# Forty-eight of 108 expert tiles computed while the token pipeline drains

## What is computed

```python
tokens = einsum('bnpd,edp->bne', patches(x, P=16, S=8), Wr) + b      # 93 tokens a row
h = tokens + attention(layernorm(tokens))                            # 8 heads of 64, causal, ALiBi
x2 = layernorm(h).reshape(-1, 128)                                   # 5952 tokens
top_vals, top_idx = top_k(x2 @ gate_weight.T, 2)
mask  = any(top_idx == e)                                            # token chose expert e
hid   = silu(einsum('td,efd->tef', x2, w1))                          # 16 experts, 512 hidden
h_mean = einsum('tef,te->ef', hid, mask) / max(counts, 1)
y_mean = einsum('ef,edf->ed', h_mean, w2)
out = h + softmax(top_vals) mixed over y_mean[top_idx]
```

## Time and profile before

| | us |
|---|---|
| median of 3 runs (lowest to highest) | 823.14 (822.13 to 823.62) |
| the profiled execution | 821.97 |
| its span, first to last instruction | 820.3 |
| TensorE busy in the span | 742.3 (90%) |
| VectorE busy | 615.6 (75%) |
| ScalarE busy | 468.0 (57%) |
| GpSimd busy | 383.2 (47%) |

### The profile page before, as it was taken

One profiled execution on the slowest core, in us unless ns is written; L12 is line 12 of the kernel. 1 busy time (PEld: TensorE's weight loads), 2 busy tenths in 40 slices (PEclk: granted clock), 3 DMA queues, 4 the chain that ended last, 5 costly groups with the idle time before them and its releaser, 6 DMA issues. The chain is left out here.

```text
span 820.3 us, 20971 instructions
## 1 busy us (share of the span) xinstructions
PE 742.3 (90%) x6670; PEld 685.7 (84%) x6670; DVE 615.6 (75%) x1621; ACT 468.0 (57%) x1021; POOL 383.2 (47%) x408
## 2 busy tenths in 40 slices
PE   5477999999999999999999999999898419999987
PEld 4466999999999999999999999998777309999983
DVE  2145788888888888888888888889986336888855
ACT  3345566656565656666566666646443108899950
POOL 3443243666555565656456565644534552222200
PEclk9798999999999999999999999999999659999989
DMA  6322123432211121112111121142000032222205
GB/s 190 105 76 54 42 67 97 135 100 52 67 50 48 47 63 51 50 47 67 51 47 47 47 71 48 32 158 77 13 13 20 20 81 73 65 64 64 64 12 149
DMA packets 42246, 53.89 MB, mean 66 GB/s; under 512 B 13651, under 2 KB 28947, under 8 KB 41680
## 3 DMA queue, kind: packets, MB, share of 16 engines
q1 hardware_dynamic: 26304, 37.13, 16.0%
q0 software_dynamic: 13120, 14.05, 6.1%
q10 hardware_dynamic: 2768, 2.00, 0.8%
HBM read 42.69 MB, written 10.26 MB: 65 GB/s over the span
## 5 line engine op out<-in xcount | busy, mean ns | idle before, releaser
L1110 POOL DMA_INDIRECT expert_rows<-hn,slot x128 | 167.5, 1309 | 64.3 <-issue 32.3
L1043 POOL TENSOR_TENSOR x_lo<-x_raw,x_hi 128x752 fp32r<-128x752 f32 x64 | 114.9, 1796 | 149.1 <-ACT x_hi L667 149.1
L831 DVE SCALAR_TENSOR_TENSOR qkv<-ps,taps,qkv 128x368 f32<-128x368 f32 x192 | 114.0, 594 | 76.8 <-ACT qkv L675 75.3
L675 ACT ACTIVATE qkv<-ps,taps 128x372 f32<-128x372 f32 x192 | 108.7, 567 | 87.5 <-PE ps L408 87.1
L834 DVE SCALAR_TENSOR_TENSOR qkv<-ps,taps,qkv 128x364 f32<-128x364 f32 x192 | 114.6, 597 | 6.8
L406 PE MATMUL ps<-x_hi,wtok_hi 128*128 128x376 f32 x256 | 94.5, 369 | 11.5 <-DVE wtok_lo L811 9.1
L500 PEld LDWEIGHTS psO<-vrow,probT 93*93 93x93 f32 x1024 | 93.4, 162 | 4.9 <-ACT probT L700 3.8
L500 PE MATMUL psO<-vrow,probT 93*93 93x65 f32 x1024 | 93.9, 245 | 2.2 <-ACT probT L700 1.1
L407 PE MATMUL ps<-x_lo,wtok_hi 128*128 128x376 f32 x256 | 88.3, 345 | 0.0
L408 PE MATMUL ps<-x_hi,wtok_lo 128*128 128x376 f32 x256 | 88.3, 345 | 0.0
L998 DVE TENSOR_REDUCE qkv<-qkv 128x512 f32 (+1 forms) x108 | 72.4, 681 | 18.1 <-ACT qkv L771 17.3
(11 more groups left out here) (160 smaller groups left out, 1607.1 us busy)
## 6 DMA issues: line engine op xcount, KB each, us to landing
x_raw<-in_x SPq DMA_DIRECT2D x64, 376.0 KB, 3.2
w1s<-in_w POOLq DMA_DIRECT2D x8, 512.0 KB, 4.8
w<-in_w SPq DMA_DIRECT2D x4, 1024.0 KB, 10.3
xs<-expert_rows SPq DMA_DIRECT2D x54, 64.0 KB, 1.8
xs<-expert_rows POOLq DMA_DIRECT2D x54, 64.0 KB, 2.1
out<-resid SPq DMA_DIRECT2D x16, 160.0 KB, 2.4
expert_rows<-hn,slot POOLq DMA_INDIRECT x128, 3.5
qkv<-in_w_tok ACTq DMA_DIRECT2D x4, 256.0 KB, 6.7
```

The source lines that it names most:

```text
L675: nc.scalar.activation(qkv[u][:, k, :, :], psP[(k + 1) % 2][:, 0:GT].rearrange("p (b n) -> p b n", n=NT), ACT.Copy, scale=taps[:, k, 2:3]) ...
L831: nc.vector.scalar_tensor_tensor(dst[:, :, 1:NT], src[:, :, 0:NT - 1], taps[:, k, 1:2], dst[:, :, 1:NT], ALU.mult, ALU.add).then_inc(tap1_ ...
L1043: nc.gpsimd.tensor_tensor(x_lo[u][:, 0:PIECE], x_raw[u][:, :], x_hi[u][:, 0:PIECE].bitcast(F32), ALU.subtract)\
L1110: nc.gpsimd.indirect_dma_start(rows, bass.IndirectOffsetOnAxis(slot[1 - u][:, c:c + 1], 0), hn[1 - u][:, c % GB, :], None)\
```

## The change

`EARLY` = 48 tiles are computed before the second part. After eleven groups (`FULL_AFTER`) the ranks tell how many full tiles each expert has already; VectorE makes a first table of these in step 15 (`early_piece`), TensorE turns it into a row in step 16, and VectorE copies it to `tab_e`. The 48 tiles are worked in twelve quads of four. Quads 0 to 3 stand in the sub-steps of step 18, 4 to 6 in step 19, and 7 to 11 (`LAST_QUADS`) after the pipeline's last step. All 48 are fetched by SP alone (`fetch_early`), from the end of the projections on, since buffers share memory with the projection's. For the same reason the last megabyte of w2 is loaded then. A quad has one bank for its four transposes and one copy (`quad_copy`), and two score banks (`psP`), which the drain leaves free, where the second part has four. The final table, five operations longer, leaves out the tiles done and numbers the other 60 from 48 on.

```diff
@@ constants and buffers @@
+ROUND, QUAD = 12, 4
+FULL_AFTER = 11
+EARLY = 48
...
+        xs = [sb(f"xs{k}", [128, D]) for k in range(NR)]
+        xsQ = [sb(f"xsQ{u}", [D, QUAD * 128]) for u in range(2)]
+        xsT = [xsQ[0][:, k * 128:(k + 1) * 128] for k in range(NX)]
@@ fetch_early @@
+        def fetch_early(eng):
+
+            eng.wait_ge(early_table, 1)
+            for u in range(2):
+                eng.wait_ge(scattered[u], 16 * 2 * GB * ((FULL_AFTER + 1 - u) // 2))
+
+            def fetch(i, k):
+                start = eng.value_load(tab_e[0:1, bass.ds(i, 1)], min_val=0, max_val=E * CAP)
+                wait(eng, xs_tr, i - (NR - 1))
+                eng.dma_start(xs[k][:, :], rows[bass.ds(start, 128), :]).then_inc(xs_early[k], 16)
+
+            for k in range(NR):
+                fetch(k, k)
+            with eng.Fori(1, EARLY // NR) as r:
+                for k in range(NR):
+                    fetch(r * NR + k, k)
+
@@ expert, quads @@
         def expert(eng, copy, i, k, done):
 
-            at = eng.value_load(tab[0:1, bass.ds(i + 128, 1)], min_val=0, max_val=(E - 1) * F)
+            table = tab_e if isinstance(i, int) and i < EARLY else tab
+            at = eng.value_load(table[0:1, bass.ds(i + 128, 1)], min_val=0, max_val=(E - 1) * F)
             wait_apart(eng, up_mm, i - (NX - 1))
             copy(wtile[k % NX][:, :], w1s[:, bass.ds(at, F)]).then_inc(done, 1)
+
+        def early_quad(t, s):
+
+            return isinstance(t, int) and t >= NG + 2 and {(NG + 2, 0): 0, (NG + 2, 1): 1, (NG + 2, 2): 2, (NG + 2, 3): 3,
+                                                          (NG + 3, 0): 4, (NG + 3, 2): 5, (NG + 3, 3): 6}.get((t, s), -1)
+
+        LAST_QUADS = range(7, EARLY // QUAD)
+
+        def quad(t, s):
+
+            q = early_quad(t, s)
+            return None if q is False or q < 0 else q
@@ SP @@
             sp.wait_ge(tap_mm, NPIECE)
-            for j in range(FB):
+            for j in range(FB - 1):
                 sp.dma_start(w2s[j][:, :, :], w2[:, j, :, :]).then_inc(late_w_in, 16)
             sp.wait_ge(zeros_ready, 1)
             sp.dma_start(rows[E * CAP:ROWS, :], zeros[:, :]).then_inc(zero_tile_out, 16)
+            sp.wait_ge(proj_mm, NG * NBLK)
+            sp.dma_start(w2s[FB - 1][:, :, :], w2[:, FB - 1, :, :]).then_inc(late_w_in, 16)
+            fetch_early(sp)
             sp.wait_ge(tail_ready, 1)
             tails(sp, 0)
             fetch_tiles(sp, 0)
@@ TensorE @@
+            def turn_quad(q):
+
+                wait(pe, xs_evac, QUAD * q)
+                for c in range(QUAD):
+                    i = q * QUAD + c
+                    pe.wait_ge(xs_early[i % NR], 16 * (i // NR + 1))
+                    nc.tensor.transpose(psTok[:, c * 128:(c + 1) * 128], xs[i % NR][:, :], ident[:, :]).then_inc(xs_tr, 1)
+
+            def up_quad(q, first, count):
+
+                for c in range(first, first + count):
+                    i = q * QUAD + c
+                    weights_ready(i // ROUND, i % ROUND)
+                    pe.wait_ge(xs_evac, QUAD * (q + 1))
+                    wait(pe, silu_done, i - 1)
+                    if i < 2:
+                        pe.wait_ge(conv_done, NG * NBLK)
+                    for j in range(FB):
+                        mm = nc.tensor.matmul(psP[i % 2][:, j * 128:(j + 1) * 128], wtile[i % NX][:, j * 128:(j + 1) * 128],
+                                              xsQ[q % 2][:, c * 128:(c + 1) * 128], start=True, stop=True)
+                    mm.then_inc(up_mm, 1)
...
+                    if q is not None and (f.attn or s == 0):
+                        turn_quad(q)
                     if prev:
 
                         pe.wait_ge(p_evac, n * 2)
@@ -527,6 +605,8 @@
                         proj(t, u, f, 3 * s + 1)
                     if f.tok:
                         tok_taps(t, s, 1, 2)
+                    if q is not None and f.attn:
+                        up_quad(q, 0, 3)
                     if f.attn and prev:
                         pe.wait_ge(v_evac, n + 1)
...
+                    if q is not None and f.attn:
+                        up_quad(q, 3, 1)
                     if prev:
...
@@ -583,25 +679,29 @@
             pe.wait_ge(tcol_ready, 1)
             pe.wait_ge(rwT_evac, NG)
             for c in range(2):
-                mm = nc.tensor.matmul(psTok[0:1, c * 128:(c + 1) * 128], tcol[:, c:c + 1], ident[:, :],
+                mm = nc.tensor.matmul(psV[0:1, c * 128:(c + 1) * 128], tcol[:, c:c + 1], ident[:, :],
                                       start=True, stop=True)
             mm.then_inc(table_mm, 1)
+            for q in LAST_QUADS:
+                if q == LAST_QUADS[0]:
+                    turn_quad(q)
+                up_quad(q, 0, 2)
+                if q + 1 in LAST_QUADS:
+                    turn_quad(q + 1)
+                up_quad(q, 2, 2)
+            pe.wait_ge(table_ready, 1)
@@ ScalarE @@
+            def quad_copy(q):
+
+                ac.wait_ge(xs_tr, QUAD * (q + 1))
+                wait(ac, up_mm, QUAD * (q - 1))
+                nc.scalar.activation(xsQ[q % 2][:, :], psTok[:, :], ACT.Copy).then_inc(xs_evac, QUAD)
+
+            def silu_quad(q, first, count):
+
+                for c in range(first, first + count):
+                    i = q * QUAD + c
+                    ac.wait_ge(up_mm, i + 1)
+                    wait(ac, tile_sum, i - (NX - 1))
+                    nc.scalar.activation(act[i % NX][:, :], psP[i % 2][:, :], ACT.Silu).then_inc(silu_done, 1)
+                    if i + NX < EARLY and copies(i + NX):
+                        expert(ac, lambda d, w: nc.scalar.activation(d, w, ACT.Copy), i + NX, i + NX, w_act_ready)
...
+                    q = quad(t, s)
+                    if q == 0:
+                        ac.wait_ge(early_table, 1)
+                        ac.wait_ge(expert_w_in, 16 * 2 * GB)
+                        ac.wait_ge(v_tr, (NG - 1) * GB)
+                        ac.wait_ge(s_mm, (NG - 1) * GB)
+                        for k in range(NX):
+                            if copies(k):
+                                expert(ac, lambda d, w: nc.scalar.activation(d, w, ACT.Copy), k, k, w_act_ready)
...
+                    if q is not None and (f.attn or s < 3):
+                        quad_copy(q)
+                        if f.attn:
+                            silu_quad(q, 0, 3)
...
+                    if q is not None and f.attn:
+                        silu_quad(q, 3, 1)
+                    if q is not None and not f.attn and s < 3:
+                        silu_quad(q, 0, QUAD)
                     if f.gate and s == 3:
                         wait(ac, gap_done, t - 3)
                         nc.scalar.activation(egap[:, :], gap[:, :], ACT.Exp).then_inc(egap_done, 1)
+                    if q is not None and not f.attn and s == 3:
+                        quad_copy(q)
+                        silu_quad(q, 0, QUAD)
...
             run(ac, step)
             ac.wait_ge(tail_ready, 1)
             tails(ac, 1)
+            for q in LAST_QUADS:
+                if q == LAST_QUADS[0]:
+                    quad_copy(q)
+                silu_quad(q, 0, 2)
+                if q + 1 in LAST_QUADS:
+                    quad_copy(q + 1)
+                silu_quad(q, 2, 2)
@@ VectorE @@
+            def sum_quad(q):
+
+                for c in range(QUAD):
+                    i = q * QUAD + c
+                    tile_total(i, i % NX)
+                    if i + NX < EARLY and not copies(i + NX):
+                        expert(dve, nc.vector.tensor_copy, i + NX, i + NX, w_dve_ready)
...
+                    if f.gate and s == 3 and not f.attn:
+                        sum_quad(quad(t, 2))
                     if f.gate and s == 3:
                         rank(t - 4, u)
                     if f.proj:
                         conv(t, u, 3 * s + 1)
                     if f.proj:
                         conv(t, u, 3 * s + 2)
+                    if q is not None and f.attn:
+                        if q == 0:
+                            first_weights()
+                        sum_quad(q)
                     if prev:
                         dve.wait_ge(out_mm, n)
                         res = resid[:, bass.ds((n - 1) * D, D)]
                         nc.vector.tensor_tensor(res, psWout, res, ALU.add).then_inc(res_add, 1)
                     if f.gate and s == 2:
                         route(t - 4)
+                    if isinstance(t, int) and t == NG - 1:
+                        early_piece(s)
+                    if isinstance(t, int) and t == NG and s == 2:
+                        dve.wait_ge(early_mm, 1)
+                        nc.vector.tensor_copy(tab_e[:, :], psTok[0:1, 0:2 * 128]).then_inc(early_table, 1)
...
+            link(nc.vector.reciprocal(invc[:, :], invc[:, :]))
+            sum_quad(LAST_QUADS[0] - 1)
             dve.wait_ge(table_mm, 1)
...
```

(3 more changed lines are left out.)

133 lines of the change are left out of this document (101 added, 32 removed).

## The result

The change makes the kernel slower: 837.5 us, median of 4 runs (836.4 to 838.8), against 823.4 for the kernel before, run beside it. The ratio is 1.016, with a 95% interval of 1.0136 to 1.0184. The forecast was 830.7: the right side, inside the range, and 6.8 us short. The profiled execution took 836.8 us with a span of 835.1, against a span of 820.3.

What follows compares the result with a forecast made beforehand. TensorE bounds the dense stretches, with some 65 us of partial use before the second part. Terms 1.0 + 3.6 + 21.0 + 2.0 + 29.8 - 49.9 sum to +7.5 us: 830.7 us by the median, range 814 to 843.

Steps and rivals of the forecast that it cites:

- The forecast case: Whole kernel: the drain's added costs exceed the gain of the moved tiles, 830.7 us, slower by 0.9%; chance 0.55.
- early table, to the last projection: Step 15: twenty small dependent VectorE operations exceed its slack, and a table copy in step 16; +1.0 us, bounds 0 and 4.
- first fetch: Start of step 18: SP fetches only after w2's last megabyte is issued, delaying the value product; +3.6 us, 2 to 7.5.
- step 18, four quads: Four sub-steps grow from 27.1 to 48.1 us, table loads standing before the exponentials; +21.0 us, floor 12.3, ceiling 27.
- clock in step 18: Sub-step 0: two idle stretches, 3.6 and 2.5 us, bring a few microseconds at half clock; +2.0 us, bounds 0 and 4.
- last value product to second part: End of the drain: quads, tail writes and fetches delay the second part's first transpose; +29.8 us, bounds 24 and 35.
- 48 tiles leave the second part: Second part: 48 tiles at 1.04 us each no longer run there; -49.9 us.
- Rivals A: Drain: engines absorb silus, loads and totals, only TensorE's added work lengthens steps; faster, 814.5 us; chance 0.25.
- rival B: Drain: each table switch blocks for twice its row, on eight of ten loads; +10 us, 841 us; chance 0.10.
- The 60.7: After the last group: end of the last five quads, in us counted from the last value product.
- the 66.1: Second part's first transpose, in us from the last value product, after SP's tail writes and first fetch; 36.3 before.
- Rival C: Costs and gain cancel: first fetch in time, clock holds, last quads at 4.15 us; 823.3 us; chance 0.10.

Runs made afterwards that it cites:

- table_only: The kernel before with only the early table added (its VectorE operations, two TensorE products and copy), which nothing reads: 826.7 us, ratio 1.0036.
- fetch_first: The changed kernel with the first six fetches ahead of w2's last megabyte and VectorE's first weight copies ahead of sub-step 0's attention: 826.3 us, ratio 1.0017.
- drop18: The changed kernel with 24 early tiles, none in step 18: three quads in step 19, three after the last group: 822.2 us, ratio 0.9968.
- no_switch: The changed kernel with plain copies instead of silu in quads 0 to 6, so ten table loads fall away: 829.7 us, ratio 1.0076.
- the kernel with both edits: The changed kernel with first fetches and first weights moved ahead, and tail writes twelve on GpSimd, four on SP, none on ScalarE: 818.0 us, ratio 0.9924.
- fetch_only: The changed kernel with only the first six early fetches put ahead of the projections' wait and w2's last megabyte: 831.5 us, ratio 1.0091.
- weights_only: The changed kernel with only VectorE's first weight copies moved ahead of the attention of step 18's sub-step 0: 834.5 us, ratio 1.0129.
- tails_pool12: The changed kernel with twelve tail writes on GpSimd behind its scatters, four on SP, none on ScalarE: 829.1 us, ratio 1.0058.

## Why the prediction was right, and by how much each step missed

The forecast case happened: ten more table loads, a first sub-step longer than the others and these near 11 us, a wait for the first fetch, five quads behind ScalarE's tail writes, a gap of 5.3 us before the second part. By the traces:

| term | predicted | measured |
|---|---|---|
| early table, to the last projection | +1.0 | +2.9 |
| first fetch | +3.6 | +3.5 |
| step 18, four quads | +21.0 | +20.8 |
| clock in step 18 | +2.0 | +5.8 |
| last value product to second part | +29.8 | +32.7 |
| 48 tiles leave the second part | -49.9 | -50.9 |
| sum | +7.5 | +14.8 |

- **Early table.** Under-sized. The last projection came at 611.25 instead of 608.39; of these 2.9 us, 0.6 stood there before the early table, at the value product of 475.06 (475.64 in the change), so that 2.3 are its own. I charged what VectorE's slack did not hold, 1.0; table_only shows 2.1 in its trace and 3.0 in its time. What failed is the thought that slack inside a sub-step absorbs a burst: at the place shown VectorE's slack was one wait of 0.49 us for ScalarE, against six operations of 0.2 us put in front of it. For the other sub-steps this is not shown.
- **First fetch.** Right: the value product came at 618.41, 6.3 us later than in the earlier trace rows, of which 2.9 are the delay before. The fetch landed before its megabyte would have (10.3 us).
- **Step 18.** The sub-steps were worked out as 13.9, 12.0, 11.0 and 11.2 us. With the clock's part taken out they were 13.9 (18.2 less 4.3), 12.4, 11.1 (as in fetch_first) and 10.6. That the load lies in front of the exponentials, what else each engine does meanwhile and in which order, could be read from the order of instructions and today's durations. Rivals A and B both fell on this, A by drop18, B by no_switch. By its time alone rival B, at 841, was nearer to 837.5 than the forecast; what rules it out is the 1.5 and 1.3 us that a load gave back. The Trainium skill's page ScalarE: Activation LUTs (What ACT_TABLE_LOAD costs) gives 2.66 us for a switch with its drain; here the load's 1.28 is what the path paid.
- **Clock.** The step that failed most. I gave 2.0, with a bound of 4, from two idle stretches that I had named; it was 5.8. The stretches came where forecast, the first shorter (1.9 us of waiting, the rest of the 3.5 being mostly the quad's transposes, at half clock) and the second 2.6, but half clock then lasted for most of sub-step 0 (0.67 in the window, 4.3 us), and came back in sub-step 2 (1.5 us), which I had not thought of.
- **From the last value product on.** The assumption that failed is that TensorE is at full clock for quads 4 and 5. The rows spoke against it already: in the kernel before the clock was at 0.82 from 637.7 to 645.1 and at 0.50 by 643, which is where quad 4 was to run. In the change the window has 0.78, and the 32 matmuls of quads 4 and 5 take 5.6 us each, where two runs of 16 take 2.0 each in the last quads. So the final counts were ready 26.0 us after the last value product (698.08), not 22.4. What followed came later with them, though not step by step as worked out: ScalarE's tail writes began at 31.5 (predicted 26.9), were shorter (7.8 us) and ended at 39.3 (35.7); the five quads took 24.4 us (24.3); SP's tail writes began at 57.1 (52.3) and took 8.0 us (9.4); the first transpose came at 69.0 (66.1). The 60.7 that I gave for the end of the quads doesn't follow from its terms, 35.7 + 22.5 + 1.8, which make 60.0; the 66.1 doesn't rest on it.
- **Gain.** Right within 1 us: 94.0 us from the first transpose to the end, against 144.9.

Rival C, in which costs and gains cancel, needed the fetch in time, full clock and quads at 4.15. The kernel with both edits shows that the two stalls and the wait behind the tail writes were removable, and went beyond it: 818.0, with a clock that was still lowered in sub-step 2.

Little of this was luck: the errors did not cancel. Early table, clock and the end of the drain each cost more than I gave, by 1.9, 3.8 and 2.9 us, and only the gain made up for some, by 1.0. So the direction was right by the mechanism, and of the 14.8 us above no change I had half.

Two things stay open. Why the clock is lowered in sub-step 2 (0.86) in the change, fetch_only, weights_only, tails_pool12 and the kernel with both edits, but not in fetch_first or no_switch, whose TensorE does the same work there, isn't told by any run. It may differ from execution to execution: the mean granted clock of the kernel before lay between 0.952 and 0.962 in the 21 runs beside table_only. And the last quads were not tried with fetches shared between two queues, so that 5 us a quad is SP's pace is read from the waits and not tested.

## What to carry to other kernels

Partly idle engines do not mean that a chain has room. Read what one more piece of work puts between two dependent steps, a table load above all, and compare the growth of the chain with what the piece is worth where it is now; here 18 us in the best case measured for 16.6, while three such pieces in a true wait, behind the last group, were a clear gain, and three more were not. Then look at each queue that the new work shares: three of the change's costs were a small thing (a copy, a fetch, the first weights) that stood behind a large one, and each was cured by another order or another queue. Last, price a new idle stretch of two or three microseconds at more than its length: here TensorE paid for it again at half clock.

## What the hardware showed that I had not expected

- Half clock followed even short idling. In sub-step 0 of the change, waits of 1.9 and 2.6 us were followed by half clock that cost 4.3 us more. In sub-step 2, where TensorE is busy 11.4 of 12.5 us with no wait above 1.2 us, the clock was at 0.86 for the window.
- A tail write, with the load of its address, takes 0.55 us on GpSimd (6.67 us for twelve), 1.00 on SP (8.02 for eight) and 0.98 on ScalarE (7.81 for eight); in the kernel before it took 1.18 on SP and 1.08 on ScalarE. The engine that no tail write was given to was the cheapest place for them, and it waits after its last scatter anyway.
